# Mixture of experts in a one-core Mamba and transformer kernel: three routing chunks under way, expert results added into the output by an indirect DMA, expert weights fetched from DRAM for every tile

## What is computed

```python
h = x + _attention(_rmsnorm(x, ln1_w), wq, wk, wv, wo)
h = h + _moe(_rmsnorm(h, ln2_w), gate_w, w1, w2, w3)
# _moe: xf is 4096 tokens x 256, E = 8 experts, inner width 512
logits = xf @ gate_w.T
rw, sel = top_k(logits, 2); rw = softmax(rw)
for e in range(E):
    we = sum(where(sel == e, rw, 0.0), axis=-1)
    out = out + (silu(xf @ w1[e].T) * (xf @ w3[e].T)) @ w2[e].T * we[:, None]
```

## Time and profile before

| | us |
|---|---|
| median of 3 runs (lowest, highest) | 3339.76 (3338.06, 3340.56) |
| the profiled execution, its own time | 3338.2 |
| its span in the trace | 3336.7 |
| PE busy | 2885.8 (86%) |
| DVE busy | 2463.1 (74%) |
| ACT busy | 1954.1 (59%) |
| POOL busy | 1090.8 (33%) |

### The profile page before, as it was taken

The page is one execution under the profiler, slowest core; times in us unless marked ns, Lnnn a source line. Parts: engine busy times, 40 slices in busy tenths (PEclk is TensorE's granted clock), DMA queues, the critical chain, the costliest instruction groups (busy, mean ns, idle before and its releaser), DMA issues. The chain is left out here.

```text
span 3336.7 us, 48301 instructions
## 1 busy us (share of the span) xinstructions
PE 2885.8 (86%) x14320; PEld 1233.6 (37%) x14321; DVE 2463.1 (74%) x2747; ACT 1954.1 (59%) x3515; POOL 1090.8 (33%) x652
## 2 busy tenths in 40 slices
PE   5798998889877758999999999999999963899990
PEld 1234434334323431222222222222222252899980
DVE  0599999999998558888888888888888365233323
ACT  3566656655643325888787878787887810344430
POOL 1788779778773450000000000000000036100107
PEclk8899999999998877999999999999999975999995
DMA  1111111111110542111111111111111036111114
GB/s 43 39 51 43 46 54 48 42 54 51 39 44 22 161 144 39 39 37 37 35 39 39 39 40 39 36 32 35 30 38 35 1 118 249 50 47 47 47 41 150
DMA packets 123096, 185.29 MB, mean 56 GB/s; under 512 B 30224, under 2 KB 77968, under 8 KB 122896
## 3 DMA queue, kind: packets, MB, share of 16 engines
q1 hardware_dynamic: 109072, 142.95, 15.0%
q0 software_dynamic: 13824, 39.86, 3.8%
HBM read 138.01 MB, written 44.43 MB: 55 GB/s over the span
## 5 line engine op out<-in xcount | busy, mean ns | idle before, releaser
L1529 DVE TENSOR_REDUCE nmh<-ring 128x2 f32<-128x1024 f32 x1024 | 1196.0, 1219 | 196.1 <-PE ring L1406 195.9
L1387 ACT ACTIVATE prob<-s_ps 128x512 f32<-128x512 f32 x2048 | 1072.9, 602 | 282.5 <-PE s_ps L1427 282.5
L767 DVE TENSOR_TENSOR_SCAN h<-dA,state,bx 128x512 f32<-128x512 f32 x512 | 618.9, 1269 | 124.7 <-ACT dA L606 124.6
L391 POOL TENSOR_TENSOR bx<-u,bb 128x2048 f32<-128x2048 f32 x128 | 578.9, 4527 | 198.1 <-DVE h L767 198.0
L1427 PE MATMUL s_ps<-qs,ks 98*128 98x512 bf16 x2048 | 613.9, 387 | 17.2 <-issue 11.5
L1439 PE MATMUL acc<-prob,vst 128*32 128x512 f32 x4096 | 550.4, 610 | 0.2 <-ACT prob L1387 0.2
L606 ACT ACTIVATE dA<-dt,aneg 128x512 f32<-128x512 f32 x512 | 348.7, 691 | 269.1 <-DVE h L767 269.0
L673 PE MATMUL y_ps<-h,ident 128*128 128x512 f32 x1024 | 495.7, 630 | 0.0
L1406 PE MATMUL ring<-k,q 64*128 64x512 bf16 x2048 | 348.0, 395 | 43.4 <-DMA k<-parts 23.7
L1427 PEld LDWEIGHTS s_ps<-qs,ks 98*128 98x128 bf16 x2048 | 149.3, 97 | 581.4 <-ACT prob L1387 466.3
L673 PEld LDWEIGHTS y_ps<-h,ident 128*128 128x128 f32 x1024 | 208.1, 203 | 234.2 <-issue 228.3
(11 more groups left out here) (222 smaller groups left out, 2634.4 us busy)
## 6 DMA issues: line engine op xcount, KB each, us to landing
bb<-b_rows SPq DMA_DIRECT2D x128, 256.0 KB, 3.1
q<-parts SPq DMA_DIRECT2D x256, 64.0 KB, 2.1
parts<-part POOLq DMA_DIRECT2D x48, 256.0 KB, 3.1
qs<-parts SPq DMA_DIRECT2D x192, 64.0 KB, 2.8
ks<-parts SPq DMA_DIRECT2D x192, 64.0 KB, 2.8
xt<-slots_in POOLq DMA_DIRECT2D x72, 128.0 KB, 2.6
slots_out<-yt SPq DMA_DIRECT2D x72, 128.0 KB, 1.8
k<-parts SPq DMA_DIRECT2D x256, 32.0 KB, 2.0
```

The source lines that it names most:

```text
L391: nc.gpsimd.tensor_tensor(bx[:, n % BR], u[:, b], bb[:, n % RB, None, :].to_broadcast([P, KI, CH]), ALU.mult).then_inc(s_bx, 1)
L767: nc.vector.tensor_tensor_scan(h[:, n % HR, d, :], dA[:, d % 2, :], bx[:, n % BR, d, :], state[:, b, n, d:d + 1], ALU.mult, ALU.add).then_ ...
L1387: nc.scalar.activation(prob[:, k % PR, j, :], s_ps[:, tile % SR, :], ACT.Exp, scale=SC).then_inc(s_exp, 1)
L1529: nc.vector.tensor_reduce(nmh[:, slot, t, 2 * s:2 * s + 2], ring[:, s, :, :], AX.X, ALU.max, negate=True).then_inc(s_free[s], 1)
```

## The change

Four things change in `moe_stage`, and nothing ahead of it but the order of the axes of `att`.

1. **Routing order.** Three chunks are under way: `hc` and `xr` have three buffers, and the scaled rows `g` four. PE transposes straight out of `att`; POOL's copy is gone, and in the loop POOL only sends scatters. ACT scales the rows once (with logarithm and exponential in place of the root), DVE no longer does. A row of `slots_in` now is 265 numbers wide: 256 features, 8 shares (one for each expert) and the number of the token. DVE works out the shares in each chunk.
2. **Base and output.** The sum `hc + xr` goes to the output tensor in DRAM at once (SP, one store of 512 KB for each chunk). The output tensor has 128 rows more, which rows without a token are added into.
3. **Weights.** Only `w2` is loaded once (one expert in each chunk). `w1` and `w3` of each tile's expert are fetched from DRAM by SP, 2 x 512 KB for each of the 72 tiles, four tiles ahead. The copies by ACT and DVE are gone.
4. **Adding up.** DVE multiplies each result with its row's share, and POOL adds the 128 rows of a tile into the output with one indirect DMA that accumulates, one after the other. An add is issued behind the load of seven tiles later (BEHIND = 7; WR, the buffers of weights, is 4). On DVE `pick`, which reads share and token out of the loaded rows, is the last thing in a step, behind `midT`. The stage "Output" is gone, and so are the eight scatters of zero rows on POOL, which SP now does as plain stores.

```diff
@@ routing, SP @@
+                def front(c):
+                    b, i = where(c)
+                    r = c % FR
+                    wait(sp, s_g, c - FR + 1)
+                    wait(sp, s_bst[r], 16 * (c // FR))
+                    for dst, src in ((hc, f_dram), (xr, x1_dram)):
+                        sp.dma_start(dst[:, r], src[b, i * CH:(i + 1) * CH, :].rearrange("(t p) e -> p t e", p=P)
+                                     ).then_inc(s_f[r], 16)
+                def keep_base(c):
+                    wait(sp, s_base, c + 1)
+                    sp.dma_start(rows_of(c), xr[:, c % FR]).then_inc(s_bst[c % FR], 16)
...
+                for c in range(NC):
+                    keep_base(c)
+                    if c + 1 < NE:
+                        expert_weights(c + 1)
+                    if c + FR < NC:
+                        front(c + FR)
+                sp.wait_ge(s_behind, 1)
+                for e in range(NE):
+                    row = sp.value_load(behind[0:1, e:e + 1], min_val=0, max_val=NE * REG)
+                    sp.dma_start(xg_dram[bass.ds(row, P), :], zero[:, :]).then_inc(s_clear, 16)
@@ routing, POOL @@
+                for c in range(NC):
+                    pool.wait_ge(s_g, c + 1)
+                    pool.wait_ge(s_share, N_SHARE * (c + 1))
+                    pool.wait_ge(s_row, c + 1)
+                    for t in range(TT):
+                        for k in range(2):
+                            nc.gpsimd.indirect_dma_start(
+                                out=xg_dram[:, :],
+                                out_offset=bass.IndirectOffsetOnAxis(ap=row_in[:, c, k, t:t + 1], axis=0),
+                                in_=g[:, c % GR, t, :], in_offset=None).then_inc(s_sc[c % GR], 16)
@@ routing, PE @@
+                for c in range(NC):
+                    logits(c)
+                    if c + 2 < NC:
+                        project(c + 2)
+                    if c + 1 < NC:
+                        turn_rows(c + 1)
+                    if c + 3 < NC:
+                        turn_attention(c + 3)
+                    ranks(c)
@@ routing, DVE @@
+                for c in range(NC):
+                    choose(c)
+                    if c + 2 < NC:
+                        add(c + 2)
+                        moments(c + 2)
+                    shares(c)
+                    if c + 2 < NC:
+                        base(c + 2)
+                    places(c)
@@ tiles, POOL @@
-                def load(j, slot, n):
+                def load(j, slot):
                     row = pool.value_load(first_row[0:1, bass.ds(j, 1)], min_val=0, max_val=NE * REG)
-                    wait_apart(pool, s_xp, j - 3, s_sc)
+                    wait(pool, s_xp, j - 3)
+                    wait(pool, s_pick, j - 3)
                     nc.gpsimd.dma_start(xt[:, slot, :], xg_dram[bass.ds(row, P), :]).then_inc(s_xt[slot], 16)
+                def add_to_out(j, slot):
+                    wait(pool, s_yt, j + 1)
+                    wait(pool, s_y, 16 * j)
+                    nc.gpsimd.indirect_dma_start(
+                        out=out[:, :], out_offset=bass.IndirectOffsetOnAxis(ap=token[:, slot:slot + 1], axis=0),
+                        in_=yt[:, slot, :], in_offset=None, compute_op=ALU.add).then_inc(s_y, 16)
+                for j in range(NJ):
+                    load(j, j % 4)
+                    if j >= BEHIND:
+                        add_to_out(j - BEHIND, (j - BEHIND) % 4)
+                for j in range(NJ - BEHIND, NJ):
+                    add_to_out(j, j % 4)
+                pool.wait_ge(s_y, 16 * NJ)
@@ tiles, SP @@
+                def weights(j, slot):
+                    e = expert_of(sp, j)
+                    wait_apart(sp, s_up, j - WR + 1, s_we)
+                    for k, w in ((0, w1T), (1, w3T)):
+                        sp.dma_start(wu[:, slot, k], w[bass.ds(e, 1)].rearrange("o (k p) n -> p (o k) n", p=P)
+                                     ).then_inc(s_wu[slot], 16)
@@ tiles, DVE @@
+                def pick(j, slot, taken, e):
+                    wait(dve, s_xt[slot], 16 * (taken + 1))
+                    wait(dve, s_y, 16 * (j - 3))
+                    nc.vector.tensor_copy(share[:, slot:slot + 1], xt[:, slot, bass.ds(e + DM, 1)])
+                    nc.vector.tensor_copy(token[:, slot:slot + 1], xt[:, slot, TOK:W]).then_inc(s_pick, 1)
                 def take_y(j, q, n):
                     slot, taken = at(q, n, 2)
                     wait(dve, s_dn, j - 1)
-                    wait(dve, s_y[slot], 16 * taken)
-                    nc.vector.tensor_copy(yt[:, slot, :], o_ps[:, q % 2, 0:DM]).then_inc(s_yt, 1)
+                    wait(dve, s_pick, j - 1)
+                    wait(dve, s_y, 16 * (j - 5))
+                    nc.vector.tensor_scalar(yt[:, slot, :], o_ps[:, q % 2, 0:DM], share[:, slot:slot + 1], None,
+                                            ALU.mult).then_inc(s_yt, 1)
...
+                    if there(j, -1):
+                        pick(j + 1, *at(q, n, -1), e)
@@ output stage (POOL L2331, DVE L2351, SP L2364) @@
-                        nc.gpsimd.indirect_dma_start(
-                            out=ya[:, t % RG, k, :], out_offset=None, in_=y_dram[:, :],
-                            in_offset=bass.IndirectOffsetOnAxis(ap=row_out[:, k, t:t + 1], axis=0)
-                        ).then_inc(s_ya[t % RG], 16)
...
```

More of the change, by code:

```diff
@@ new lines, in _ @@
+                nc.gpsimd.memset(ones[:, :], 1.0).then_inc(s_set, 1)
+                nc.gpsimd.memset(before[:, :], 1.0).then_inc(s_set, 1)
+                nc.gpsimd.memset(zero[:, :], 0.0).then_inc(s_set, 1)
+                nc.gpsimd.memset(ident[:, :], 0.0).then_inc(s_id, 1)
+                nc.gpsimd.iota(part_no[:, :], pattern=[[0, 1]], base=0, channel_multiplier=1,
+                               allow_small_or_imprecise_dtypes=True).then_inc(s_set, 1)
+                nc.gpsimd.iota(starts[:, :], pattern=[[P, NT]], base=0, channel_multiplier=0,
+                               allow_small_or_imprecise_dtypes=True).then_inc(s_set, 1)
@@ new lines, in exponent, with take_rows @@
+                def exponent(c):
+                    wait(act, s_dif, c + 1)
+                    nc.scalar.activation(ex[:, c % 2, :], dif[:, c % 2, :], ACT.Exp).then_inc(s_ex, 1)
+                def take_rows(c):
+                    wait(act, s_t2, c + 1)
+                    wait(act, s_lg, c)
+                    for k in range(KM):
+                        nc.scalar.activation(gT[:, k, :], t2_ps[:, k, :], ACT.Identity,
+                                             scale=ln2[:, k:k + 1]).then_inc(s_gT, 1)
@@ L2068, in _, with add @@
             @block.vector
             def _(dve):
+                dve.wait_ge(s_set, SETS)
+                def add(c):
+                    r = c % FR
+                    wait(dve, s_f[r], 32 * (c // FR + 1))
+                    wait(dve, s_wo, c + 1)
+                    for half in range(2):
+                        part = flat(hc[:, r, 2 * half:2 * half + 2, :])
+                        nc.vector.tensor_tensor(part, flat(h_ps[:, 2 * half:2 * half + 2, :]), part, ALU.add
+                                                ).then_inc(s_h, 1)
@@ new lines, in _ @@
+                nc.vector.memset(one[:, :], 1.0)
+                for c in range(2):
+                    add(c)
+                    moments(c)
+                    base(c)
+                for c in range(NC):
+                    choose(c)
[6 more added lines that the diff above has]
+                    places(c)
+                nc.vector.tensor_copy(behind[:, :], count[0:1, :]).then_inc(s_behind, 1)
@@ L2195, in _ @@
-                sp.wait_ge(s_we, 16 * 3 * NE)
-                for j in range(4):
-                    store(j, j)
+                def weights(j, slot):
[4 more added lines that the diff above has]
+                                     ).then_inc(s_wu[slot], 16)
+                for j in range(WR):
+                    weights(j, j)
```

780 lines of the change are left out of this document (301 added, 479 removed).

## The result

Five runs of the changed kernel gave a median of 3323.43 us (3313.1 to 3323.7), five of the kernel before 3339.76. The ratio is 0.9942, with a 95% interval of 0.9926 to 0.9958: faster, by 0.6%. The forecast was 3232 and its range ended at 3310, so the time lies 13 us above the range, and about six sevenths of the expected gain of 107.5 us are missing. The profiled execution took 3323.58 us with a span of 3322.0.

A forecast was written before the change was run, and what follows sets the result against it. PE was taken to bound the tiles, a chain the routing, POOL's gathers mostly the output. Against 3338.2 us, -41 + 1.5 + 0 + 13 - 81 = -107.5 gave 3230.7, as a median 3232 us; range 3208 to 3310.

The forecast's parts named there:

- L: Time of a tile's add from the start of POOL's issue to its landing, put at 3.85 us.
- overlap little: +0.15: In the tiles, weight fetches and the add's data hardly coincide, adding 0.15 us to the add's 3.7 us.
- the ring: Tile loop of pick, load, add, pick, closing once a tile: 1.85 us plus L, 5.70 against PE's 5.52, +13 us.
- the tile term: First row load to end of the last yt: +14.5 us forecast for this stretch.
- A: Rival in the tiles: the add fits, L is 3.67 or less, ring hidden below PE's 5.52; 3219 or 3213 us; chance 0.20.
- C: Rival at DVE's pick: adds done row by row, L 8.5, ring 10.3, +340, 3559 us; chance 0.12.
- B: Rival in the tiles: read before write costs in full, in traffic; L 4.9, +87, 3306 us; 0.25 including what lies between.
- Weights: 0: Weight fetches in the tiles, asked for four tiles ahead by SP, are hidden and cost 0 us.
- Routing: Routing and tables: PE's operations bound a chunk at 11.0 us in place of 15.0, giving -41 us.
- half clock, -14: Rival in routing: all PE work at half clock, about 15 us a chunk, -14 in place of -41; no chance given.
- The start of the tiles: Tile stage starts 5.4 us behind the last scatter's end, as before; first product then +1.5 us for weights.
- The end: After the last yt: at most two adds outstanding, 8.3 us in place of 89.0, giving -81 us.

The follow-up runs named there:

- e9_halfproj: Changed kernel with BEHIND 5 and the routing's projection summed over one of its two halves only: 3226.17 us, 0.9657 of the kernel before.
- e5_phase: Changed kernel in which SP asks for weights after the down products of a tile, not its up products: 3263.6 us, 0.9754 of the kernel before.
- e1_deep: Changed kernel with 12 places for share and token and 8 for yt in place of 4: 3234.95 us, 0.9678 of the kernel before.
- e8_behind5: Changed kernel with BEHIND 5 in place of 7, nothing else: 3232.72 us, 0.9669 of the kernel before.
- e2_nofetch: Changed kernel that fetches weights for the first four tiles only and reuses them: 3254.32 us, 0.9729 of the kernel before.
- e4: Changed kernel with more places for share, token and yt, and no weight fetches behind the fourth tile: 3232.14 us, 0.9672 of the kernel before.
- e6: e1_deep plus 16 unused transposes of the unit matrix on PE in each routing chunk: 3238.18 us, 0.9671 of the kernel before.
- e7: e1_deep with the eight stores of zero rows shared by SP and ACT, four each: 3232.25 us, 0.9656 of the kernel before.
- e10: Changed kernel with BEHIND 5 and rows of slots_in 320 numbers wide in place of 265: 3227.12 us, 0.9674 of the kernel before.
- e3: Changed kernel with a plain indirect store in place of the accumulating add: 3227.57 us, 0.9651 of the kernel before.

## Why the prediction was wrong

**The step that failed** is the size of L, and in it one sentence: that weights "overlap little: +0.15". L was 4.9 at the median (5.09 in the mean while the ring binds) and not 3.85. The sentence reckoned from when the old kernel's PE ends its up products, and put the add's data 4 us later in a lap of 5.5, as if that distance would stay. The 72 adds of the kernel after show that it doesn't stay (distance of each add's issue from SP's nearest first fetch, and L):

| the add's issue | adds | L: median (least to most) |
|---|---|---|
| 2.7 to 1.5 us ahead of the fetch | 13 | 3.8 (3.8 to 4.1) |
| 1.5 to 0.8 ahead | 6 | 5.7 (4.3 to 5.8) |
| 0.8 ahead to 0.8 behind | 18 | 5.6 (5.3 to 6.6) |
| 0.8 to 1.5 behind | 18 | 5.0 (4.7 to 5.6) |
| 1.5 to 2.5 behind | 9 | 4.1 (3.9 to 5.0) |
| no fetch left beside it | 8 | 3.8 (3.6 to 3.8) |

L goes with the distance, and 42 of the 72 adds stood within 1.5 us of a fetch. How they come there can be followed over laps. At a distance the lap is 5.8 to 6.1 us as a rule, longer than the 5.5 in which PE asks for weights, so the add falls back against the fetch until the two meet: the adds from 2835.77 on were issued 2.64, 2.11, 1.81, 1.44 and 0.58 us ahead, and the last of these took 6.6 us. Then PE waits for the ring too, the two keep a like pace, and the distance stays within 1.3 us for many laps before it opens again. A quiet lap of the same kernel, in order of time, with the fetch 2.27 us behind the add:

```profile
3078.34 1.59 POOL L2138 DMA_INDIRECT out_x<-yt,token  x1 [0.30 <-issue]
...
3080.61 0.37 SPq L2156 DMA_DIRECT2D wu<-in_w1T  x1
...
3082.31 0.15 DVE L2192 COPY share<-xt 128x1 f32 x1 [3.77 <-DMA out_x<-yt,token]
```

The other runs fit, each with most of its adds at one distance:

| run | most adds' issue against SP's first fetch | L, median | from `yt` to `yt` |
|---|---|---|---|
| after | anywhere, 42 of 72 within 1.5 us | 4.9 | 6.68 |
| e9_halfproj | 0.7 to 1.3 behind (49) | 4.7 | PE's, 5.46 |
| e5_phase | 2.3 to 3.0 ahead (57) | 3.8 | 5.73 |
| e1_deep | 2.3 to 3.0 ahead (60) | 3.9 | PE's, 5.46 |
| e8_behind5 | 2.2 to 2.7 behind (53) | 3.9 | PE's, 5.46 |
| e2_nofetch | no fetch | 3.8 | 5.655 |

e5 moved nothing but SP's request, and L followed. Whether the delay arises in the DMA engines' queues or at the memory wasn't told apart. The Trainium skill (DMA: Bandwidth & Descriptors, Latency and other measured facts) gives 0.2 us on average and 2 at high load for an access to HBM. The traces agree in direction only, at +1.1 us of the median L, and load here means a burst at the same time and not mean traffic, since e1 has the higher mean traffic and the lower L.

**The ring itself was right**, with one term missing: lap less L is 2.02 us in the kernel after, in e2 and in e5 (5.85 - 3.83) alike, where 1.85 was summed; DVE's start behind a landing, 0.1 to 0.2, had no term. Without the burst the tile term would have been as forecast: in e2 the stretch from the first row load to the last `yt` is 420.1 us, 14.7 above before, where +14.5 was forecast. In part that is luck: laps of 5.83 and not 5.70, but some 60 of them and not 71. A (L at most 3.67) didn't hold even in the quiet: 3.8. Its support, that all transfers of 128 KB land within 1.8 to 2.8 us, also left out one in the same view, the first store of zero rows, at 6.8. C (L of 8.5, rows in series) fell wholly; the maximum of all 72 is 6.6. B was priced at 4.6 for a read and a whole write one after the other, plus 0.3 for traffic, and met the number by another split: 3.8 in the quiet and 1.1 for the weights. So its reason was wrong where its price was right. It had 0.25 for itself and what lies between; at 3306 it was inside the range, and the range was missed because the forecast's other gains, put in there in full, fell 26.6 us short, against 7.2 that came unforeseen.

**Weights: 0** was right for PE, which never shows a wait for `wu` from DMA in the stretch of the tiles, and e4 against e1 confirms it. It was wrong for the add, whose landing the ring waits for.

**Routing: -24.7, not -41.** The chunk took 13.3 us (`row_in` of the first to the last, 2696.5 to 2789.4, over 7) in place of 11.0. From the first scatter's start to the last's 101.8 us went by (2697.6 to 2799.4) where 85.9 were forecast, +15.9; the first came 35.0 us behind the stage's start and not 38.2, -3.2; from the last to the first row load it was 11.0 and not 6.7, +4.3: together 17.0, which is the forecast's own 2842.3 - 2800.6 = 41.7 less 24.7. One reading of before was off. A chunk of 15.0 is the spacing of the first scatters; `row_in` of before goes from 2714.9 to 2802.4, 12.5 us a chunk, and POOL's queue came behind it. So by `row_in` a chunk got no shorter by the change; against before the gain is an earlier first scatter, 45.5 to 35.0 us behind the stage's start, a shorter run of scatters, 110.4 to 101.8, and a shorter way from the last one to the load, 16.6 to 11.0, with the eight zero scatters gone from POOL. The step that failed is the sum of PE's operations as the bound: it took the logits at 1.95 and the projection at 5.21 and nothing for PE's waits. In the trace of after the granted clock is 0.67 in this stretch, and both the lengths and the waits differ, in order of time:

```profile
2751.23 6.61 PE L1884 MATMUL h_ps<-wo,attT 128*128 128x256 f32 x16 [0.93 <-ACT attT L1819]
2757.94 1.29 DVE L1942 TENSOR_TENSOR hc<-h_ps,hc 128x512 f32<-128x512 f32 x2 [4.50 <-PE h_ps L1884]
...
2761.51 0.30 ACT L1828 ACTIVATE m_lv<-m_mv,m_epsc 128x4 f32<-128x4 f32 x1 [1.31 <-DVE m_mv L1959]
...
2762.08 1.71 ACT L1833 ACTIVATE g<-hc,m_rs 128x256 f32<-128x256 f32 x4
2763.84 1.92 PE L1893 MATMUL t_ps<-m_ident,g 128*128 128x128 f32 x8 [1.83 <-ACT g L1833]
```

Projection, DVE's sum, ACT's scaling, PE's turn follow one on the other: three chunks under way did not take the engines out of each other's path. That the clock alone is the cause has e6 against it (0.76 and no gain beyond the scatter, but with more work on PE), that PE's work is, e9. A chain over DVE, ACT and PE is what is left, argued and not shown; which link to cut was not tried. The rival "half clock, -14" had the sign of the miss. Its 15 us don't follow from its row: 9.9 us of PE work, longer by 3.58 / 1.95, and 1.1 of waiting are 19.3; the granted clock was 0.67 on average, between the two levels. (64 scatters of 1.27 are 81.3 us and not 81.6, which changes nothing.)

**The start of the tiles** has a miss of 4 to 5 us, counted above: the first row load came 11.0 us behind the last scatter, where it was 6.4 from issue to issue before. The forecast took the old distance, 5.4 from the last one's end. In e1, e5, e6, e7, e9 and e10 it is 10.3 to 11.2; where SP's last zero store is later than that (2799.1 in e8), the load is 9.7 behind the store, at 2808.8. It isn't the division of these stores (e7) nor the row width (e10); what it is stays open.

**The end: -70.7, not -81.** From last `yt` to the end 18.3 us went by, not 8.3. The chain of work that ended last, in the kernel after, in order of time (start us, us, what):

```profile
3299.92 3.73 DMA out_x<-yt,token
...
3304.40 3.83 DMA out_x<-yt,token
...
3308.25 0.02 POOLq L30
3308.27 0.71 issue
3308.98 3.63 DMA out_x<-yt,token
...
3313.36 1.55 POOL out_x L2138
```

Three issues follow the last `yt` (3303.18), 4.4 to 4.6 us apart; the forecast counted two adds. They wait in turn since `pick` of the last tile needs no add beyond that of tile 67. The gap from landing to issue is 0.75, not 0.30. And the end comes 8.6 us behind the last issue, though an add takes 3.6 to 3.8 at this point. In e8 one issue follows the last `yt`, and 11.8 us go by; also there the end is 8.7 behind the last issue. The part beyond the landing, some 4.9 us, isn't explained; the kernel before had 3.3 us from the end of the `res` in the earlier trace rows to its own end.

**Ahead of the stage, -7.2 was not foreseen**, in code that the change doesn't touch. It is all there by 113 us, where the scan begins (120 before): the stretch from the start to 112.0 in the kernel after, and to 119.0 in that before, hold the same 130 PE instructions.

```profile
0.00:112.00 112.00, 67.39 (x130) 24.08 (x131) 8.00 (x40) 36.57 (x51) 48.48 (x30) 0.89 0.16 46
```

```profile
0.00:119.00 119.00, 74.20 (x130) 25.95 (x131) 8.01 (x40) 36.61 (x52) 49.75 (x31) 0.84 0.15 43
```

They took 67.39 us at a granted clock of 0.89 in place of 74.20 at 0.84. All eleven experiments begin the scan as early, at 111 to 113. Why the clock is higher is open, so 7 of the 15 us between the two spans came by none of the change's argued steps. The same holds for 7 of the 109.6 us between the spans of before and e8.

**The signs by which to know it** were named for the right three places. "L beyond 4.6" came in full; the adds at the end were late, three of them; the chunk at 13.3 stopped between the 11 that was to show it right and the 14 that was to show it wrong.

## What to carry to other kernels

When a change makes a loop of waits close once per tile, write its lap as a sum, and put into it what the awaited transfer takes when every burst that can run beside it falls together with it: once the lap is longer than the old bound, the distance between the two is no longer that of the old trace, and here 42 of 72 laps had them together. Ask then how many tiles the loop spans; here the position of one issue in POOL's order (BEHIND 6 or 5 in place of 7), without any memory, gave 3231 to 3233 us, 0.967 to 0.968 of the kernel before, and beats both kernels. A stage that is a chain over three engines isn't bounded by the sum of one of them, even with several chunks under way.

## What was new of the hardware

- POOL takes 1.59 us to issue an accumulating indirect DMA of 128 rows, and 0.96 to 1.00 for a plain one of the same form.
- From issue to landing the accumulating one takes 3.8 us in the quiet (e2), and 5.3 to 6.6 when it is issued within 0.8 us of the request for 1 MB on another queue (kernel after). More than 2 us from such a request it takes 3.9, and a plain store there 3.0 (e1, e3).
- The mean traffic is no measure for it: 3.9 us at 238 GB/s in e1, 4.9 at 190 GB/s in the kernel after.
- PE's granted clock in the routing followed PE's own work: 0.76 with 16 extra transposes a chunk, 0.63 to 0.69 without, 0.60 with half the projection left out. The chunk took 13.3, 12.2 to 14.5 and 13.4 us.
- Between the last transfer of a stage and what follows lay more than the transfers' own times: 10 to 11 us from the last scatter to the next stage's first load, and about 4.9 us from the last add's landing to the end.
